# Steps 0 to 12 of the final stream, set between the products of the last layer's second half

## The chip, the cores and the metric

The kernel runs on one core of a Trainium2 chip. The metric is the device time of one execution in microseconds. A core has five engines that run beside each other, each through its own list of instructions in the order written: TensorE (PE, matrix products and transposes into PSUM banks), VectorE (DVE), ScalarE (ACT), GpSimd (POOL) and SyncE (SP, which only issues transfers here). They are tied together by semaphores: an instruction that waits holds up all that stand behind it on its engine.

## The reference

Three models in a row over x of 2 sequences by 1024 tokens, each with a residual sum: a two-layer token transformer of width 192 with banded attention, a retention block of width 128, and a layer of 8 experts with one expert for each token.

```python
def _L0_tok_ref(call, ...):
    for l in range(L):
        a = _longformer_attn(x, att_mask, ...)
        x = _ln(x + a, g1[l], beta1[l])
        h = jax.nn.relu(x @ W1[l].T + b1[l]) @ W2[l].T + b2[l]
        x = _ln(x + h, g2[l], beta2[l])
    x = _ln(x, gf, betaf)
    return x @ Wc.T + bc

def _L0_attn_ref(x, ...):
    y = retention_core(layernorm(x, ln1_g, ln1_b), decay_logit, W_out, b_out, conv_w, conv_b)
    x = x + y
    h = layernorm(x, ln2_g, ln2_b)
    h = jax.nn.gelu(jnp.einsum('btd,hd->bth', h, W1) + b1, approximate=False)
    y = jnp.einsum('bth,dh->btd', h, W2) + b2
    return x + y

h = _L0_tok_ref(x, ...)
h = h + _L0_attn_ref(_layernorm(h, axis=-1), ...)
h = h + _L0_ffn_ref(_layernorm(h, axis=-1), ...)
```

## The kernel before

The tokens are cut into blocks of 128, eight (`NB`) for each of the two sequences, sixteen in all (`NN`). The layers run as four rounds, sequence 0 with layers 0 and 1, then sequence 1 with layers 0 and 1. A round ends with a stretch whose order is written out by hand as a list of pairs in `seq_c`; PE, DVE, ACT and POOL each walk the same list and do their own part of each pair:

- `("y", i)`: for i from 0 to 7 the attention's output product of a block, for i from 8 to 15 the second feed-forward product (PE, `y_block`, L1369, six products with `w2s` per block). DVE adds the residual and takes the statistics (L1084, L922 to L924), POOL raises the variance to the power -0.5 (L545).
- `("z", i)`: DVE normalizes (L928), POOL scales and shifts into `resid` (L551, L552).
- `("tr", i)`: PE transposes z for the next product.
- `("hid", i)`: a hidden product of 512 tokens (PE, L1575 and L1576, banks 6 and 7), and its Relu on ACT (L811).

A y block lies in bank i % 4, so four can be under way before a z must be done.

What the last round leaves in `resid` goes through the final stream, a software pipeline of 29 steps (`NN + DEPTH`, L1593 on PE, L1141 on DVE, L819 on ACT, L624 on POOL). In step t each stage takes the block that belongs to it: block t takes the final norm's statistics, block t-1 is normalized (z0), transposed on PE (L1607, L1608), scaled by ACT (L824, L825) and multiplied with `wca` and `wcb` (L1650, L1651), whose result ACT copies to `h0` (L842). Block t-4 is normalized and transposed (L1634), block t-5 goes through the state scan on DVE (L1185), block t-6 through the five-tap convolution (L1601, ten matmuls) and the state product (L1612), blocks t-8 to t-10 through the second norm (L1656) and the products m1 and m2 (L1627, L1619), block t-12 through the last norm (L1661), and block t-13 through the router's product (L1641). DVE's part of a step takes all statistics first, hands the variances to POOL for one power (L637), and normalizes with the power of the step before (L1193). Four times in the stream a group of blocks is routed (`choose`, `rank`, `place`), and POOL scatters the rows to DRAM. When all sixteen blocks are out there, SP loads expert tiles, and 23 tiles run through the experts.

All four engines begin the stream behind the last pair of the last round.

## Time and profile before

| | |
|---|---|
| Time, median of 3 runs | 917.97 us (917.25 to 919.37) |
| Time of the profiled execution | 919.02 us |
| Its span in the trace | 916.9 us |
| Busy in the span | PE 809.2 (88%), DVE 634.4 (69%), POOL 567.2 (62%), ACT 563.3 (61%) |
| Mean granted clock of TensorE | 0.953 of full speed |
| Chain that ended last | PE 59%, DVE 21%, issue 5%, SP's queue 4%, POOL 4%, ACT 4%, DMA 3% |

The page of the profile also shows the span in 40 slices of about 23 us each:

```profile
PE   5979998999999989989999899999998986887397
DVE  2769975547899655578997553689975436988454
PEclk8989998999999999999999999999999996997599
```

A digit is the busy share in tenths, and in the row PEclk the clock that TensorE was granted, in tenths of full speed. The last eight digits are the end of the last layer, the stream and the experts. The clock has two levels, 2.4 GHz (1.00 in the views) and 1.2 GHz (0.50).

In the rows below "idle before" in square brackets is the time that the engine stood still ahead of a row, and what ended it. A matmul's duration overlaps with the next one's, so what a group of matmuls costs is read from the start of one group to the start of the next.

### The profile page before, as it was taken

To read this page: it belongs to the slowest core of one execution; us is meant where nothing else is said; L and a number is where in the kernel's file an instruction comes from. 1 tells how busy PE (TensorE), PEld (TensorE's weight loads), DVE (VectorE), ACT (ScalarE), POOL (GpSimd) and SP (SyncE) were. 2 spreads that over 40 slices of the span, in tenths; PEclk is the share of its full clock that TensorE was granted. 3 is DMA by queue.
4 is the path that set the end of the run, shared out by engine and by line. 5 is a ranking of instruction groups with operands and counts; after the bars stand their busy time and mean duration, and the time that the engine had idled before them with its cause. 6 is when DMAs were issued, how large, how long until landed. Compare 5 with 4: busy or idle time off the path is not lost.

```text
span 916.9 us, 23665 instructions
## 1 busy us (share of the span) xinstructions
PE 809.2 (88%) x8467; PEld 617.3 (67%) x8467; DVE 634.4 (69%) x1959; ACT 563.3 (61%) x1559; POOL 567.2 (62%) x820
## 2 busy tenths in 40 slices
PE   5979998999999989989999899999998986887397
PEld 2757766576777666667776666677766664876397
DVE  2769975547899655578997553689975436988454
ACT  2858885437788853267888543778885423565164
POOL 3638885545388856475888554438885546759345
PEclk8989998999999999999999999999999996997599
DMA  2310000142000012430000024200000245001331
GB/s 65 105 47 3 4 13 11 58 139 77 6 4 3 13 35 87 114 92 26 3 3 14 11 81 116 79 5 4 3 3 2 79 121 205 1 3 41 93 103 39
DMA packets 38595, 43.84 MB, mean 48 GB/s; under 512 B 7162, under 2 KB 33881, under 8 KB 38345
## 3 DMA queue, kind: packets, MB, share of 16 engines
q1 hardware_dynamic: 18348, 19.40, 7.1%
q10 hardware_dynamic: 17860, 18.19, 6.7%
q0 software_dynamic: 2272, 4.74, 1.7%
q8 instruction: 69, 1.13, 0.5%
q14 instruction: 46, 0.38, 0.1%
HBM read 20.70 MB, written 21.59 MB: 46 GB/s over the span
## 4 chain that ended last, share of the span: by engine, by line
PE 59%; DVE 21%; issue 5%; SPq 4%; POOL 4%; ACT 4%; DMA 3%; POOLq 0%; DVEq 0%; ACTq 0%
PE bank L1369 7%; DVE p L1011 6%; DVE nmx L1002 5%; PE bank L1575 5%; PE bank L1457 5%; PE bank L1576 5%; PE bank L1506 4%; PE bank L1530 4%; PE bank L1395 3%; PE bank L1406 3%; PE bank L1460 2%; PE bank L1509 2%; PE bank L1680 2%; PE bank L1601 2%; PE bank L1689 2%
## 5 line engine op out<-in xcount | busy, mean ns | idle before, releaser
L573 POOL TENSOR_TENSOR p<-p 128x384 f16<-128x384 f32 (+1 forms) x320 | 283.8, 907 | 103.4 <-ACT p L746 98.7
L1002 DVE TENSOR_REDUCE nmx<-bank 128x1 f32<-128x384 f32 (+1 forms) x384 | 190.6, 511 | 20.7 <-PE bank L1460 16.2
L744 ACT ACTIVATE p<-bank 128x384 f32<-128x384 f32 (+1 forms) x384 | 170.9, 452 | 54.3 <-PE bank L1509 38.0
L1506 PE MATMUL bank<-stack 103*128 103x128 bf16 x1056 | 145.1, 222 | 5.6 <-DMA stack<-mtr 5.1
L746 ACT ACTIVATE p<-bank 128x384 f16<-128x384 f32 (+1 forms) x320 | 144.3, 451 | 0.0
L1509 PE MATMUL bank<-bandb,idb 128*128 128x128 bf16 x672 | 135.3, 222 | 0.0
L1530 PE MATMUL bank<-vst,p 128*128 128x49 bf16 x2112 | 115.8, 185 | 15.2 <-DVE p L1011 13.6
L1457 PE MATMUL bank<-stack 100*128 100x384 bf16 (+1 forms) x384 | 121.2, 316 | 7.3 <-DVE nmx L1002 2.9
L1530 PEld LDWEIGHTS bank<-vst,p 128*128 128x128 f16 x2112 | 89.5, 97 | 32.4 <-DVE p L1011 19.1
L1506 PEld LDWEIGHTS bank<-stack 103*128 103x128 bf16 x1056 | 88.3, 98 | 29.7 <-issue 14.5
L1460 PE MATMUL bank<-bandb,idb 128*128 128x128 bf16 x672 | 101.2, 220 | 0.0
L545 POOL TENSOR_TENSOR rstd<-ve,colc 128x1 f32<-128x1 f32 x64 | 35.2, 550 | 101.7 <-DVE ve L924 101.7
L1084 DVE TENSOR_TENSOR bank<-bank,resid 128x192 f32<-128x192 f32 x64 | 23.1, 361 | 82.8 <-PE bank L1369 82.8
L1460 PEld LDWEIGHTS bank<-bandb,idb 128*128 128x128 bf16 x672 | 66.0, 98 | 20.9 <-issue 0.8
L811 ACT ACTIVATE hid<-bank 128x512 f32<-128x512 f32 x48 | 28.7, 597 | 81.8 <-PE bank L1576 81.8
L758 ACT ACTIVATE stack<-bank 96x1024 bf16<-96x1024 bf16 x64 | 65.1, 1017 | 18.6 <-PE bank L1395 17.2
L1395 PE MATMUL bank<-idb,hid 128*96 128x128 bf16 x768 | 59.3, 221 | 10.1 <-POOL hid L590 5.2
L1369 PE MATMUL bank<-w2s,hid 128*128 128x192 f32 x384 | 65.1, 328 | 2.8 <-ACT hid L811 2.8
L1369 PEld LDWEIGHTS bank<-w2s,hid 128*128 128x128 f32 x384 | 62.3, 190 | 7.2 <-issue 7.2
L1395 PEld LDWEIGHTS bank<-idb,hid 128*96 128x96 bf16 x768 | 51.2, 124 | 23.4 <-issue 16.8
L1509 PEld LDWEIGHTS bank<-bandb,idb 128*128 128x128 bf16 x672 | 65.6, 98 | 0.7
L1011 DVE TENSOR_TENSOR p<-p 128x384 f16<-128x384 f32 (+1 forms) x64 | 63.2, 987 | 2.2
(253 smaller groups left out, 1818.0 us busy)
## 6 DMA issues: line engine op xcount, KB each, us to landing
xs<-zrow ACTq DMA_DIRECT2D x8, 2193.0 KB, 13.5
xt<-xs SPq DMA_DIRECT2D x23, 129.0 KB, 2.1
w2s<-in_w SPq DMA_DIRECT2D x4, 576.0 KB
mwbs<-in_mwb SPq DMA_DIRECT2D x1, 2064.0 KB, 8.5
mw2s<-in_mw SPq DMA_DIRECT2D x1, 2048.0 KB, 12.8
...
stack<-mtr SPq DMA_DIRECT2D x96, 3.0 KB
...
```

The source lines that it names most:

```text
L573: nc.gpsimd.tensor_tensor(p2[:, u % RING, 0:w], p32[:, u % RING, 0:w], p1[:, u % RING, 0:w], ALU.subtract).then_inc(p2_pool, 1)
L744: ins = nc.scalar.activation(p32[:, s % RING, 0:w], ps[2 + s % 3][:, 0:w], ACT.Exp)
L746: ins = nc.scalar.activation(p1[:, s % RING, 0:w], ps[2 + s % 3][:, 0:w], ACT.Exp)
L1002: nc.vector.tensor_reduce(nmx[:, vn % 3, h:h + 1], nat_bank(v)[:, 0:w], AX.X, ALU.max, negate=True).then_inc(max_done, 1)
L1011: nc.vector.tensor_tensor(p2[:, u % RING, 0:w], p32[:, u % RING, 0:w], p1[:, u % RING, 0:w], ALU.subtract).then_inc(p2_dve, 1)
L1369: ins = mm(y, hid[:, m, blk(n % BPC)], w2s[:, m, :], start=m == 0, stop=m == FF // P - 1)
L1395: ins = nc.tensor.transpose(psb[3 + (3 * b + g) % 2][0:NPIECE, blk(h)], nat[:, b % 2, g * HG + h, :], idb[:, :])
L1457: mm(s_ps[:, 0:len(win) * P], q, stack[0:K_NAT, H + h, blk(win[0], len(win))], start=True, stop=False)
L1460: ins = mm(s_ps[:, blk(i)], idb[:, :], bandb[:, 0 if m < n else 1, :], start=False, stop=(i, m) == edges[-1])
L1506: ins = mm(ps[2 + s % 3][:, blk(i)], stack[0:K_ALL, H + h, blk(m)], stack[0:K_ALL, h, blk(n)], start=True, stop=m == n)
L1509: ins = mm(ps[2 + s % 3][:, blk(i)], idb[:, :], bandb[:, 1 if m < n else 0, :], start=False, stop=True)
L1530: ins = mm(out_ps, pt[:, w % RING, blk(a)], vst[:, m, h, :], start=False, stop=i == HH - 1 and a == len(win) - 1 and pt is p2)
```

## The change

Steps 0 to 12 of the stream (`FILLED = 13`) are taken out of the loop behind the rounds and put into the list of the last round, by the table `STREAM`. There are three kinds of such steps: step 0, 1 and 2 at y9, y10 and y11, steps 3 to 8 at the six hidden products of the second half, and steps 9 to 12 at y12 to y15. Each step is cut in two. The pair `("head", t)` stands ahead of its y block or hidden product, `("rest", t)` behind it. DVE and POOL do their whole step at the head. PE's and ACT's heads hold the convolution, the first transposes, m1, m2 and the router's product, and their rests the product with `wca` and the transposes of blocks t-8 and t-12.

So that both can be under way, the banks change. In the second half of the last round a y block takes bank i % 2, and y10 to y15 wait for z of the block two before instead of four before. The stream takes banks 2 to 7 where it took 0, 1, 3, 4, 6 and 7, the router's product moves from bank 5 to 0 and `rank` from 2 to 1, and the scaled blocks go to `ata` and `atb` instead of `xa` and `xb`. First uses of banks get a wait for what was there. The stream's small tiles lie in front of the experts' in memory now. The step functions are the loop bodies of before; the diff is cut to what differs and to PE's part in full.

```diff
+FILLED = 13
...
+        def y_bank(i, last):
+
+            return ps[i % 2 if last and i >= NB else i % 4][:, 0:D]
...
+            def stream(t):
...
+                        if kind == "head":
+                            stream(j)
...
+            def stream_head(t):
+                if t == 0:
+                    nc.scalar.activation(gs[0:1, 0, 0:1], lfa[0:1, 0:1], ACT.Gelu)
+                i = t - 1
+                if 0 <= i < NN:
+                    act.wait_ge(t0_mm, i + 1)
+                    nc.scalar.activation(ata[:, blk(i % NB)], ps[4][0:DLO, 0:P], ACT.Identity, bias=lfa[:, 1:2],
...
+            def stream_rest(t):
+                i = t - 1
+                if 0 <= i < NN:
+                    act.wait_ge(hw_mm, i + 1)
+                    nc.scalar.activation(h0[:, i, :], ps[2][:, 0:DM], ACT.Copy).then_inc(kept, 1)
...
+                        if kind == "head":
+                            stream_head(i)
+                        if kind == "rest":
+                            stream_rest(i)
...
-                        y = ps[i % 4][:, 0:D]
+                        y = y_bank(i, rnd == B * L - 1)
...
+                        if kind == "head":
+                            stream(i)
...
             def y_block(i):
                 n = block_of(i)
+                last = rnd == B * L - 1
                 if i >= 4:
-                    pe.wait_ge(z_ready, at(z_ready, i - 3))
-                y = ps[i % 4][:, 0:D]
+                    pe.wait_ge(z_ready, at(z_ready, i - 1 if last and i >= NB + 2 else i - 3))
+                y = y_bank(i, last)
...
+            def stream_head(t):
+                i = t - 6
+                if 0 <= i < NN:
+                    b, n = divmod(i, NB)
+                    pe.wait_ge(a1_done, min(i + 2, (b + 1) * NB))
+                    if i:
+                        pe.wait_ge(y_added, i)
+                    else:
+                        pe.wait_ge(z_ready, START[z_ready.num][B * L - 1] + NB)
+                    for k in range(KC):
+                        mm(ps[3][:, 0:DM], xn[:, b, n * P + k:(n + 1) * P + k], diag[:, k, :], start=k == 0, stop=False)
+                i = t - 1
+                if 0 <= i < NN:
+                    pe.wait_ge(z0_ready, i + 1)
+                    if i == 0:
+                        pe.wait_ge(ln_out, START[ln_out.num][B * L - 1] + NB)
+                    if t - 9 >= 0:
+                        pe.wait_ge(a2_done, t - 8)
+                    nc.tensor.transpose(ps[4][0:DLO, 0:P], z0[:, i % 2, 0:DLO], idf[:, :])
+                    nc.tensor.transpose(ps[4][0:DHI, P:2 * P], z0[:, i % 2, DLO:D], idf[:, :]).then_inc(t0_mm, 1)
+                i = t - 6
+                if 0 <= i < NN:
+                    pe.wait_ge(scan_done, i + 1)
+                    mm(ps[3][:, 0:DM], st[:, i % 4, :], wos[:, :], start=False, stop=True).then_inc(c_mm, 1)
+                i = t - 10
+                if 0 <= i < NN:
+                    pe.wait_ge(gelu_done, i + 1)
+                    if i:
+                        pe.wait_ge(x_added, i)
+                    else:
+                        pe.wait_ge(h_relu, START[h_relu.num][B * L])
+                    for m in range(2):
+                        ins = mm(ps[7][:, 0:DM], gl[:, i % 2, m, :], aw2s[:, m, :], start=m == 0, stop=m == 1)
+                    ins.then_inc(m2_mm, 1)
+                i = t - 9
+                if 0 <= i < NN:
+                    pe.wait_ge(a2_done, i + 1)
+                    if i:
+                        pe.wait_ge(gelu_done, i)
+                    else:
+                        pe.wait_ge(h_relu, START[h_relu.num][B * L] - 1)
+                    for m in range(2):
+                        ins = mm(ps[6][:, blk(m)], aw1s[:, m * P:(m + 1) * P], ht[:, i % 2, :], start=True, stop=True)
+                    ins.then_inc(m1_mm, 1)
+                i = t - 4
+                if 0 <= i < NN:
+                    pe.wait_ge(z1_ready, i + 1)
+                    if t - 13 >= 0:
+                        pe.wait_ge(a3_done, t - 12)
+                    nc.tensor.transpose(ps[5][:, 0:P], z1[:, i % 2, :], idf[:, :]).then_inc(t1_mm, 1)
+                i = t - 13
+                if 0 <= i < NN:
+                    pe.wait_ge(a3_done, i + 1)
+                    if i == 0:
+                        pe.wait_ge(z_ready, START[z_ready.num][B * L])
+                    for g, (a, _) in enumerate(GROUPS):
+                        if g and i == a:
+                            pe.wait_ge(lg_read, g)
+                    ins = mm(ps[0][:, i * E:(i + 1) * E], xm[:, i % 2, :], wgs[:, :], start=True, stop=True)
+                    if i + 1 in [e for _, e in GROUPS]:
+                        ins.then_inc(lg_mm, 1)
+
+            def stream_rest(t):
+                i = t - 1
+                if 0 <= i < NN:
+                    pe.wait_ge(a0_done, i + 1)
+                    if i:
+                        pe.wait_ge(kept, i)
+                    else:
+                        pe.wait_ge(z_ready, START[z_ready.num][B * L - 1] + NB - 1)
+                    mm(ps[2][:, 0:DM], ata[:, blk(i % NB)], wca[:, :], start=True, stop=False)
+                    mm(ps[2][:, 0:DM], atb[0:DHI + 1, blk(i % NB)], wcb[0:DHI + 1, :], start=False, stop=True).then_inc(hw_mm, 1)
+                i = t - 8
+                if 0 <= i < NN:
+                    pe.wait_ge(z2_ready, i + 1)
+                    pe.wait_ge(a0_done, min(t, NN))
+                    nc.tensor.transpose(ps[4][:, 0:P], z2[:, i % 2, :], idf[:, :]).then_inc(t2_mm, 1)
+                i = t - 12
+                if 0 <= i < NN:
+                    pe.wait_ge(z3_ready, i + 1)
+                    pe.wait_ge(a1_done, min(t - 3, NN))
+                    nc.tensor.transpose(ps[5][:, 0:P], trow[:, i, 0:DM], idf[:, :]).then_inc(t3_mm, 1)
...
-            for t in range(NN + DEPTH):
...
+            for t in range(FILLED, NN + DEPTH):
+                stream_head(t)
+                stream_rest(t)
...
+STREAM = {("y", 9): (0,), ("y", 10): (1,), ("y", 11): (2,), ("hid", 6): (3,), ("hid", 7): (4,), ("hid", 8): (5,),
+          ("hid", 9): (6,), ("hid", 10): (7,), ("hid", 11): (8,), ("y", 12): (9,), ("y", 13): (10,), ("y", 14): (11,),
+          ("y", 15): (12,)}
+
+
 def seq_c(rnd):
+    if rnd == B * L - 1:
+        seq = []
+        for kind, i in _seq_c():
+            if kind == "tr" and i >= NB:
+                continue
+            steps = STREAM.get((kind, i), ())
+            seq += [("head", t) for t in steps]
+            seq.append((kind, i))
+            seq += [("rest", t) for t in steps]
+        return seq
     last = rnd % L == L - 1
     seq = []
     for kind, i in _seq_c():
```

PE's list from y9 to the first hidden product. In it `bank0<-w2s,hid` with two rows is a y block, `z0` the normalized block of a step, `wca,ata` the product of its transposes. Before:

```order
L1369 MATMUL bank1<-w2s,hid 128x192 [waits h_relu,z_ready]
L1369 MATMUL bank1<-w2s,hid 128x192 x5
L1369 MATMUL bank2<-w2s,hid 128x192 [waits h_relu,z_ready]
L1369 MATMUL bank2<-w2s,hid 128x192 x5
L1369 MATMUL bank3<-w2s,hid 128x192 [waits h_relu,z_ready]
L1369 MATMUL bank3<-w2s,hid 128x192 x5
L1575 MATMUL bank6<-xa,w1a 128x512 [waits h_relu,ln_out]
L1576 MATMUL bank6<-xb,w1b 128x512
```

After (y9, head 1, y10, rest 1, head 2, y11; L1398 is the y block's line now):

```order
L1398 MATMUL bank1<-w2s,hid 128x192 [waits h_relu,z_ready]
L1398 MATMUL bank1<-w2s,hid 128x192 x5
L1419 MATMUL bank4<-idf,z0 96x128 [waits ln_out,z0_ready]
L1420 MATMUL bank4<-idf,z0 96x128
L1398 MATMUL bank0<-w2s,hid 128x192 [waits h_relu,z_ready]
L1398 MATMUL bank0<-w2s,hid 128x192 x5
L1471 MATMUL bank2<-wca,ata 128x128 [waits z_ready,a0_done]
L1472 MATMUL bank2<-wcb,atb 128x128
L1419 MATMUL bank4<-idf,z0 96x128 [waits z0_ready]
L1420 MATMUL bank4<-idf,z0 96x128
L1398 MATMUL bank1<-w2s,hid 128x192 [waits h_relu,z_ready]
L1398 MATMUL bank1<-w2s,hid 128x192 x5
```

The transposes of z0 and the product with `wca` stand between the y blocks now, and y10 is in bank 0 where y8 was.

DVE's list from the second half's second y block on. Before (y9, z8, y10):

```order
L1084 TENSOR_TENSOR bank<-bank,resid 128x192 [waits resid_ready,y_mm]
L922 BN_STATS bnst<-bank 128x6 [waits dve_own]
L923 BN_AGGR mv<-bnst 128x2 [waits dve_own]
L924 TENSOR_SCALAR ve<-mv 128x1 [waits dve_own]
L928 TENSOR_SCALAR zt<-bank,mv,rstd 128x192 [waits y_rstd,resid_ready,z_mm]
L1084 TENSOR_TENSOR bank<-bank,resid 128x192 [waits resid_ready,y_mm]
```

After, from the end of step 0 over y9 and z8 to z0 of step 1 (L974 to L1010 are the stream's lines):

```order
L992 TENSOR_SCALAR vin<-mean 128x1
L1187 TENSOR_TENSOR bank<-bank,resid 128x192 [waits resid_ready,y_mm]
L944 BN_STATS bnst<-bank 128x6 [waits dve_own]
L945 BN_AGGR mv<-bnst 128x2 [waits dve_own]
L946 TENSOR_SCALAR ve<-mv 128x1 [waits dve_own]
L950 TENSOR_SCALAR zt<-bank,mv,rstd 128x192 [waits y_rstd,resid_ready,z_mm]
L974 BN_STATS sums<-resid 128x6 [waits resid_ready]
L989 BN_AGGR mean<-sums 128x2 [waits dve_own]
L989 BN_AGGR mean<-sums 128x2 x3
L991 TENSOR_SCALAR vin<-mean 128x4 [waits dve_own]
L992 TENSOR_SCALAR vin<-mean 128x1
L1010 TENSOR_SCALAR z<-resid,mean,rs 128x192 [waits rs_ready]
```

Step 1's statistics and z0 stand behind y9 and z8 now, and step 0's between y8 and y9.

PE's list at y14 and y15 before, with the first product of the stream behind them:

```order
L1369 MATMUL bank2<-w2s,hid 128x192 [waits h_relu,z_ready]
L1369 MATMUL bank2<-w2s,hid 128x192 x5
L1369 MATMUL bank3<-w2s,hid 128x192 [waits h_relu,z_ready]
L1369 MATMUL bank3<-w2s,hid 128x192 x5
L1607 MATMUL bank0<-idf,z0 96x128 [waits z0_ready]
L1608 MATMUL bank0<-idf,z0 96x128
L1650 MATMUL bank6<-wca,xa 128x128 [waits a0_done]
```

After, from the convolution of head 11 to y14:

```order
L1411 MATMUL bank3<-diag,xn 128x128 [waits y_added,a1_done]
L1411 MATMUL bank3<-diag,xn 128x128 x4
L1419 MATMUL bank4<-idf,z0 96x128 [waits a2_done,z0_ready]
L1420 MATMUL bank4<-idf,z0 96x128
L1424 MATMUL bank3<-wos,st 128x128 [waits scan_done]
L1433 MATMUL bank7<-aw2s,gl 128x128 [waits x_added,gelu_done]
L1433 MATMUL bank7<-aw2s,gl 128x128
L1443 MATMUL bank6<-ht,aw1s 128x128 [waits gelu_done,a2_done]
L1443 MATMUL bank6<-ht,aw1s 128x128
L1450 MATMUL bank5<-idf,z1 128x128 [waits z1_ready]
L1398 MATMUL bank0<-w2s,hid 128x192 [waits h_relu,z_ready]
```

Between y13 and y14 PE now has a whole head, whose first row waits for DVE's add of step 11 (`y_added`) and whose transposes wait for its `z0`, and y14 stands behind all of it.

## Rows read from the trace of the kernel before

**Rows 1.** Timeline of PE: start us, duration us, what, idle before.

```profile
727.42 8.04 PE L1369 MATMUL bank<-w2s,hid 128*128 128x192 f32 x48 [0.34 <-ACT hid L811]
...
735.30 1.02 PE L1575 MATMUL bank<-xa,w1a 96*128 96x512 f32 x2
...
761.00 0.45 PE L1607 MATMUL bank<-idf,z 128*96 128x128 f32 x1 [6.41 <-DVE z L1193]
...
799.20 1.34 PE L1601 MATMUL bank<-diag,xn 128*128 128x128 f32 x10
800.38 0.27 PE L1607 MATMUL bank<-idf,z 128*96 128x128 f32 x1
```

**Rows 2.** Busy time in the stretch of steps 1 to 12: PE, PEld, DVE, ACT, POOL, clock.

```profile
761.00:799.20 38.20, 31.19 (x199) 26.70 (x200) 29.92 (x158) 19.55 (x58) 24.79 (x36) 0.79 0.22 83
```

**Rows 3.** Timeline of DVE at y11, z10 and z11.

```profile
735.50 0.37 DVE L1084 TENSOR_TENSOR bank<-bank,resid 128x192 f32<-128x192 f32 x1 [0.34 <-PE bank L1369]
...
736.63 0.48 DVE L928 TENSOR_SCALAR zt<-bank,mv,rstd 128x192 f32<-128x192 f32 x1
737.43 0.48 DVE L928 TENSOR_SCALAR zt<-bank,mv,rstd 128x192 f32<-128x192 f32 x1 [0.33 <-POOL rstd L545]
```

**Rows 4.** Timeline of DVE: steps 0 and 2 of the stream.

```profile
757.10 0.07 DVE L1097 MEMSET vin<- 128x10 f32 x1
...
758.80 0.14 DVE L1175 TENSOR_SCALAR vin<-mean 128x1 f32<-128x1 f32 x1
...
760.86 0.35 DVE L1157 BATCH_NORM_STATS2 sums<-resid 128x6 f32<-128x192 f32 x1
...
761.81 0.37 DVE L1193 TENSOR_SCALAR z<-resid,mean,rs 128x192 f32<-128x192 f32 x1
```

**Rows 5.** Timeline of DVE: first add and z0 of steps 10 and 14.

```profile
786.14 0.29 DVE L1147 TENSOR_TENSOR x<-bank,x 128x128 f32<-128x128 f32 x1
...
788.07 0.35 DVE L1193 TENSOR_SCALAR z<-resid,mean,rs 128x192 f32<-128x192 f32 x1
...
801.17 0.29 DVE L1147 TENSOR_TENSOR x<-bank,x 128x128 f32<-128x128 f32 x1
...
803.59 0.35 DVE L1193 TENSOR_SCALAR z<-resid,mean,rs 128x192 f32<-128x192 f32 x1
```

**Rows 6.** Timeline of PE: a convolution at low clock, a step at full clock.

```profile
773.83 2.34 PE L1601 MATMUL bank<-diag,xn 128*128 128x128 f32 x10
775.96 0.42 PE L1607 MATMUL bank<-idf,z 128*96 128x128 f32 x1
...
796.41 0.27 PE L1607 MATMUL bank<-idf,z 128*96 128x128 f32 x1
...
796.85 0.61 PE L1619 MATMUL bank<-aw2s,gl 128*128 128x128 f32 x4
...
797.86 0.39 PE L1650 MATMUL bank<-wca,xa 96*128 96x128 f32 x2
...
798.30 0.28 PE L1656 MATMUL bank<-idf,z 128*128 128x128 f32 x1
```

**Rows 7.** Windows: busy times; the third last figure is the granted clock.

```profile
61.00:66.00 5.00, 4.42 (x30) 3.23 (x30) 2.25 (x5) 2.99 (x11) 2.38 (x4) 0.50 0.01 1
393.00:400.00 7.00, 5.02 (x39) 3.15 (x38) 3.67 (x10) 4.46 (x9) 6.26 (x13) 1.00 0.27 74
579.00:582.00 3.00, 3.00 (x20) 2.39 (x19) 1.85 (x5) 2.34 (x5) 0.64 (x2) 0.50 0.18 60
760.00:776.00 16.00, 10.97 (x43) 8.67 (x44) 9.67 (x53) 6.08 (x17) 10.44 (x13) 0.50 0.59 221
```

**Rows 8.** Timeline of PE: gaps elsewhere in the program.

```profile
61.58 0.39 PE L1506 MATMUL bank<-stack 103*128 103x128 bf16 x2 [4.74 <-DMA stack<-mtr]
...
395.87 0.62 PE L1395 MATMUL bank<-idb,hid 128*96 128x128 bf16 x8 [1.98 <-POOL hid L590]
...
577.71 0.62 PE L1395 MATMUL bank<-idb,hid 128*96 128x128 bf16 x8 [1.60 <-POOL hid L590]
```

355 lines of the change are left out of this document (145 added, 210 removed).

## The prediction, made before the changed kernel ran

> **What bounds the kernel now.** I read the timeline of TensorE (PE) first, since the change moves its work, from the first feed-forward product of the last layer's second half to the experts [rows 1]. Here y8 to y11 (L1369) start at 727.42 and the six hidden products after them at 735.30, so a y block costs 7.88 / 4 = 1.97 us. The engine is nearly full until y15 ends at 754.59 (761.00 less 6.41). Then come 6.41 us without a matmul, until VectorE (DVE) has the first row of the stream: that idle time is what one would like to fill. The stream's step 13 begins on PE at 799.20 and its z transpose (L1607, which I call T0) at 800.38. **All steps that move lie between 754.6 and 799.2, 44.6 us**, and all that stands behind T0 of step 13 is unchanged. The question is only when that T0 comes.
>
> The stage view [rows 2] shows two engines nearly full in those 38.2 us of steps: PE 31.2 and DVE 29.9. That speaks against a simple overlap. A step is no spare PE work. It is a chain DVE, POOL, DVE, PE, ScalarE (ACT), PE. The DVE timeline gives the pieces: a y block's add, statistics and epsilon take 1.13 us until its neighbour's z can start [rows 3], begin 0.20 after PE is done (735.50 against 735.30), and a z takes 0.48, or 1.28 for the last two of a group, where the second waits for POOL's power. Steps 0, 1 and 2 [rows 4]: step 0 takes DVE 757.10 to 758.95, 1.85 us; a small step takes 1.32 from its first statistic (760.86) to the end of its z (762.18). A step 7 to 10 takes 2.29 from its first add to the end of z0 (786.14 to 788.43), one from 11 on 2.7 (801.17 to 803.95, less a pause of 0.1) [rows 5].
>
> **What the change costs, with the clock as it is now.** Every head is put ahead of a y block on both engines. So PE's y10 stands behind T0 of step 1, T0 waits for z0 of DVE's step 1, and that stands behind DVE's y9, which waits for PE's y9. In the order of before the y blocks ran back to back and DVE followed. Now each y block waits for DVE's answer to the y block before it. I walk along it.
> - y8 ends on PE at 727.42 + 1.97 = 729.39. DVE: 0.20, y8 1.13, step 0 1.85, y9 1.13, z8 0.48, step 1 1.32, which gives 735.50. T0 at 735.55, two transposes 0.22 (half of the 0.44 from 796.41 to 796.85 [rows 6]), y10 at 735.77. PE has done nothing since 731.36: **a gap of 4.19 us**.
> - y10 to y11: 1.97 + 0.20 + 1.13 + 0.48 + 1.32 + 0.05 + 0.22 = 5.37. y11 runs 741.14 to 743.11.
> - y11 to the hidden products: 0.20 + 1.13 + 1.28 + step 3 (1.32, and 0.27 for a second statistic) + 0.05 + 0.22 = 4.48. They start at 747.59 and not at 735.30, 12.3 us late for three steps.
> - Here the overlap is real. A hidden product is 1.72 us of PE (10.32 / 6) that needs no DVE, and ACT's copies of T0 hide behind it. The convolution is 1.18 (799.20 to 800.38 [rows 1]), T0 0.22, the state product 0.22, m2, m1 and one transpose 1.01 together (796.85 to 797.86), so some 0.45, 0.45 and 0.11, the two products of T0's copies 0.44 (797.86 to 798.30) [rows 6]. Hidden 10.32, rests of steps 3 to 8 2.75, heads 4 to 8 5.85, head 9 2.18: 21.1 us. DVE needs 1.6 (step 3) to some 3.2 (step 8, z0 at 2.29 and three more of 0.3) beside PE's 2.4 to 4.0, so PE sets the time. y12 starts at 768.7.
> - y12 to y15 stand against steps 10, 11 and 12. y12 to y13: 1.97 + 0.20 + 1.13 + 2.29 + 0.05 + 1.45 (T0 to the end of the head, 796.41 to 797.86 [rows 6]) = 7.1. The next two: 1.97 + 0.20 + 1.13 + 0.48 + 2.7 + 0.05 + 1.45 = 8.0 each. The convolution and the rests fit into this, and so do ACT and POOL, which were busy for 19.6 and 24.8 us of 38.2 in the steps alone [rows 2]. y15 ends at 768.7 + 7.1 + 16.0 + 1.97 = 793.8.
> - From there 0.20 + 1.13 + 1.28 + 0.1 (three small fills) + 2.7 + 0.05: T0 of step 13 at 799.2 against 800.4, **a gain of 1.2 us** out of 44.6.
>
> Costed at nothing: the bank numbers; the activation tables (one load for Gelu, as before); the copies to ata and atb for xa and xb; the queues. ACT issues its two fills of xs ahead of step 1's copies, which come 6 us later. SP's three loads of expert weights wait for the last y block and so start 39 us later, near 794. They are wanted after the last routing step, some 50 us behind step 13's T0; a load longer than that would hold up the experts, us for us.
>
> The Trainium skill (Perfetto Trace Analysis, Optimization Strategy) says that regimes with different busiest engines may gain from being interleaved. By it the PE work of steps 0 to 12 would go where PE waits. The stage rows speak against it here: DVE is as full in the steps as PE, and the order hands each y block the other engine's latency.
>
> **The clock.** A gap of 4.19 us is new, and one of about 2.7 us follows behind y10, one of 3.8 behind y11. Each loop of y12 to y15 holds some 1.5 and 1.2 us of idle time with the convolution between. What rows show of such gaps [rows 7, 8]: after 4.74 us (until 61.58) the granted clock was 0.50; after 6.41 it was 0.50 from 760 to 776; after 1.60 us (577.71) it was 0.50 from 579 to 582; after 1.98 us (395.87) it stayed at 1.00. So after 4.19 us I take 1.2 GHz as near certain and for the later loops as about even. The price: ten convolution matmuls span 2.13 us at the low level (773.83 to 775.96 [rows 6]) and 1.18 at the full one, nearly double.
> - y10 and y11 at half speed: 2 x 1.97, and the T0 pairs 2 x 0.22: **+4.4**. The rests lie in gaps.
> - The hidden products start low. In the solid work from 773.83 the level rose at about 776.9, so a low stretch of 3.4 us in solid work: **+1.7**. If it lasts twice as long, +3.4.
> - In y12 to y15 one more such stretch, of which PE works two thirds: **+1.1**. Bounds: none, 0; every loop low, 3 x 3.4 (1.97 + 1.45 doubled) = +10.
>
> The Trainium skill (TensorE: Matmul & The Clock Gate, Why this matters for your kernels) advises against idle gaps between bursts of matmuls, since the clock drops. The trace agrees at 4.74 and 6.41 us and shows a drop at 1.60 too, so I do not rely on the page's size of gap.
>
> **Sum.** -1.2 + 4.4 + 1.7 + 1.1 = +6.0 us. The profiled execution took 919.02 (span 916.9), which gives 925.0; it lies 1.05 above the median of 917.97, so on the scale of the medians **924.0 us**.
>
> **Rivals.**
> - The clock holds, or drops once and briefly. Then only -1.2 to +1 remains: 916.8 to 919. For it: the gap of 1.98 us left the clock alone. Against it: this gap is twice as long, 4.19 us in one piece, and two more follow. It decides at y10: if y10 lasts 1.97 us, this is the case. With the sum off by 0.7 us it is faster than before, and so it is the case on the other side of slower.
> - The overlap works as meant: DVE's z is there before PE asks, and PE's own work sets the end. PE's work in steps 0 to 12 is 12 x (0.22 + 0.44), 7 convolutions and states at 1.40, 9 + 5 + 1 transposes at 0.11 and 7 m products at 0.45: 22.5 us. With 754.6 and DVE's 5.5 us behind y15 that puts T0 of step 13 at 782.6, 17.8 earlier: 900 us. It needs y10 not to stand behind T0 of step 1; the order of the instructions says that it does.
> - The clock stays low through the second half too: y12 to y15 in loops of 11.4 us instead of 8.0, +10 in place of +1.1: 930 to 933.
> - DVE has slack in the loops that I did not see (adds that run while PE still works on the y block): up to 0.5 us in each of six loops, 3 us less with the clock as forecast: 921.
>
> **Chances.** Forecast with its neighbours (920 to 929): 0.60. Clock holds or nearly: 0.18, split evenly over its bound, since 0.2% is 1.84 us, about what a measurement of this kernel can tell from no change. Low throughout, over 929: 0.10. Overlap as meant or another gain of over 2 us: 0.12. So faster 0.20 (0.12 and 0.08 of the clock that holds), same 0.15 (the other 0.10, and 0.05 of the forecast's neighbours), slower 0.65. The range 915.5 to 930.5 leaves out the overlap as meant and the worst of the low clock. The forecast's own range is 920 to 928.
>
> **What would show it.** y9 on PE followed by about 4 us of idle time put down to DVE's z; y10 lasting near 3.9 us and a granted clock of 0.5 around 736 to 750; the first hidden product 12 to 17 us later than 735.3; y12 to y15 starting 7 to 8 us or more apart, with DVE's first add of a step directly behind its y block; then steps of about 4 us as before. Wrong would be a y10 that starts right behind y9, or a T0 of step 13 before 795 or behind 812.

## The result, and the profile after

The changed kernel takes 925.67 us (median of 4 runs, 923.50 to 927.12); the kernel before took 917.61 beside it (4 runs, 914.34 to 919.37). The ratio is 1.009, with a 95% interval of 1.0053 to 1.0127: **8.1 us slower**. The prediction was 924.0, slower, 6.0 us more. The profiled execution took 923.50, its span is 921.3.

By the two profiles the whole of it lies in one stretch, from the start of y8 to T0 (the z transpose on TensorE, PE) of step 16. In the timeline of PE of the changed kernel (start us, duration us, what, idle time before it and what ended it; T0 is now L1419, the y block L1398, the hidden product L1691):

```profile
723.39 4.14 PE L1398 MATMUL bank<-w2s,hid 128*128 128x192 f32 x24 [0.34 <-ACT hid L859]
731.22 0.45 PE L1419 MATMUL bank<-idf,z 128*96 128x128 f32 x1 [3.69 <-DVE z L1010]
...
738.45 0.45 PE L1419 MATMUL bank<-idf,z 128*96 128x128 f32 x1 [2.77 <-DVE z L1010]
...
746.68 0.45 PE L1419 MATMUL bank<-idf,z 128*96 128x128 f32 x1 [3.98 <-DVE z L1010]
...
747.14 1.92 PE L1691 MATMUL bank<-xa,w1a 96*128 96x512 f32 x2
...
770.26 2.12 PE L1398 MATMUL bank<-w2s,hid 128*128 128x192 f32 x12
...
777.54 2.12 PE L1398 MATMUL bank<-w2s,hid 128*128 128x192 f32 x12
...
785.74 2.12 PE L1398 MATMUL bank<-w2s,hid 128*128 128x192 f32 x12
...
795.11 2.57 PE L1398 MATMUL bank<-w2s,hid 128*128 128x192 f32 x12
...
803.49 0.45 PE L1419 MATMUL bank<-idf,z 128*96 128x128 f32 x1 [1.54 <-DVE z L1010]
...
808.75 0.27 PE L1419 MATMUL bank<-idf,z 128*96 128x128 f32 x1
...
816.69 0.27 PE L1419 MATMUL bank<-idf,z 128*96 128x128 f32 x1
```

and of the kernel before, y12 and T0 of steps 14 and 16 (y8 and step 13 are in [rows 1]):

```profile
746.56 3.65 PE L1369 MATMUL bank<-w2s,hid 128*128 128x192 f32 x21 [0.78 <-ACT hid L811]
...
804.35 0.27 PE L1607 MATMUL bank<-idf,z 128*96 128x128 f32 x1
...
812.28 0.27 PE L1607 MATMUL bank<-idf,z 128*96 128x128 f32 x1
```

From y8 to T0 of step 16 it was 812.28 - 727.42 = 84.9 us and is 816.69 - 723.39 = 93.3: 8.4 us more. Behind that T0 both kernels need the same 104.6 us (916.9 - 812.28 and 921.3 - 816.69), so the expert weights, which SyncE now fetches from 797.71 us on instead of 754.63, hold up nobody. Ahead of y8, where the two programs do the same, the changed kernel happens to be 4 us earlier in its profile; y8 started between 721.1 and 729.9 in the profiles of this study. That scatter is why a stretch is compared below, beside the time of the whole.

The busy times of the stretch from y8 to T0 of step 13 say it shortest (start:end, length, then busy us of PE, PE's weight loads, DVE, ACT, POOL, granted clock, DMA share, GB/s), before first:

```profile
727.42:800.38 72.96, 58.77 (x330) 47.88 (x330) 46.09 (x223) 26.33 (x71) 41.37 (x63) 0.88 0.39 127
```

```profile
723.39:803.49 80.10, 58.73 (x330) 49.54 (x330) 47.28 (x223) 26.00 (x71) 40.32 (x63) 0.89 0.24 74
```

The same 330 matmuls keep PE busy for the same 58.8 us, and it stands idle for 21.4 us instead of 14.2. Nothing was overlapped on balance; idle time was only moved, and 7 us added. The granted clock is 0.88 before and 0.89 after. So the changed kernel does not do more of this work at the low level than the kernel before, which had its low stretch in the first steps of the stream (0.50 from 760 to 776, [rows 7]); it does it in other places. What is called the price of the clock below is therefore counted against the changed kernel at full clock, and not against the kernel before. The waits of PE in the changed kernel from 723 to 808 name what it waits for:

```profile
PE bank L1419 <- DVE z L1010: 15.2, 7, 4.0
PE bank L1411 <- DVE x L964: 6.1, 4, 2.2
```

Seven waits for VectorE's (DVE's) z0 and four for its add (L964) ahead of the convolution (L1411), 21.3 us. Both stand in DVE's order behind its work on a y block. At y13, in the timeline of DVE (add of y13, add of step 11, z0 of step 11):

```profile
779.70 0.37 DVE L1187 TENSOR_TENSOR bank<-bank,resid 128x192 f32<-128x192 f32 x1 [2.90 <-PE bank L1398]
...
781.22 0.28 DVE L964 TENSOR_TENSOR x<-bank,x 128x128 f32<-128x128 f32 x1
...
783.76 0.44 DVE L1010 TENSOR_SCALAR z<-resid,mean,rs 128x192 f32<-128x192 f32 x1
```

DVE first idles for 2.90 us for PE's y13, and then PE idles for DVE. Behind y15 it is the same, and there DVE's part is the longer one: the add of y15, the add of step 13 and z0 of step 13, for which T0 of step 13 waits:

```profile
797.72 0.37 DVE L1187 TENSOR_TENSOR bank<-bank,resid 128x192 f32<-128x192 f32 x1 [4.31 <-PE bank L1398]
...
800.16 0.28 DVE L964 TENSOR_TENSOR x<-bank,x 128x128 f32<-128x128 f32 x1
...
802.99 0.44 DVE L1010 TENSOR_SCALAR z<-resid,mean,rs 128x192 f32<-128x192 f32 x1
```

The granted clock (the third figure from the end) in y10, and in y15 with its head:

```profile
731.20:735.20 4.00, 3.98 (x16) 3.97 (x17) 0.00 (x0) 0.80 (x2) 1.01 (x1) 0.58 1.09 305
...
792.44:797.50 5.06, 5.06 (x25) 5.06 (x26) 0.97 (x4) 1.77 (x5) 1.01 (x1) 0.66 0.00 0
```

### The profile page after: what moved, and what is told of

Read it like the earlier page. It is cut to its first block, busy times and chain, and to the rows that moved or that the text cites. A ratio compares the mean times of both kernels' runs of the same rounds, so it can differ in the third digit from the quotient of the medians.

```text
span 921.3 us, 23671 instructions
## 1 busy us (share of the span) xinstructions
PE 808.4 (88%) x8467; PEld 619.2 (67%) x8467; DVE 636.3 (69%) x1959; ACT 562.6 (61%) x1559; POOL 567.6 (62%) x820
## 4 chain that ended last, share of the span: by engine, by line
PE 59%; DVE 23%; issue 5%; SPq 4%; POOL 4%; ACT 3%; DMA 2%; POOLq 0%; DVEq 0%; ACTq 0%
PE bank L1398 7%; DVE p L1114 6%; PE bank L1569 5%; PE bank L1691 5%; PE bank L1692 5%; DVE nmx L1105 4%; PE bank L1618 4%; PE bank L1642 4%; PE bank L1507 3%; PE bank L1518 3%; PE bank L1572 2%; PE bank L1621 2%; PE bank L1730 2%; PE bank L1739 2%; SPq L462 2%
## 5 line engine op out<-in xcount | busy, mean ns | idle before, releaser
L1187 DVE TENSOR_TENSOR bank<-bank,resid 128x192 f32<-128x192 f32 x64 | 23.1, 361 | 90.6 <-PE bank L1398 90.6
L1398 PE MATMUL bank<-w2s,hid 128*128 128x192 f32 x384 | 69.0, 338 | 2.0 <-ACT hid L859 2.0
L1398 PEld LDWEIGHTS bank<-w2s,hid 128*128 128x128 f32 x384 | 65.6, 199 | 5.6 <-issue 5.6
```

The costliest lines, as they stand in the source:

```text
L1398: ins = mm(y, hid[:, m, blk(n % BPC)], w2s[:, m, :], start=m == 0, stop=m == FF // P - 1)
```

## The experiments

My theory: the place of the steps in the order makes a closed loop of PE and DVE at every y block (each waits for the other's last piece of work), and its gaps lower the clock. The rivals: the pair of PSUM banks that the y blocks now share holds them; or a step's own chain is too long for this place, whatever the order. All kernels at one glance; the stretch goes from y8 to T0 of step 16 in each one's profile, the last column is the ratio to the kernel before, measured on the same chip in the same rounds. The runs were made on several chips, and the median of the kernel before lay between 917.1 and 922.9 us beside them. So medians of different rows are compared by their ratios, or put on the scale of 917.6 us.

| kernel | y8, T0 of 16 | stretch us | against before | ratio (95%) |
|---|---|---|---|---|
| before | 727.42, 812.28 | 84.9 | | |
| changed | 723.39, 816.69 | 93.3 | +8.4 | 1.009 (1.0053 to 1.0127) |
| vector ahead | 726.20, 797.54 | 71.3 | -13.5 | 0.9837 (0.9799 to 0.9876) |
| third bank | 723.45, 816.68 | 93.2 | +8.4 | 1.0081 (1.0046 to 1.0115) |
| gaps filled | 729.26, 820.37 | 91.1 | +6.3 | 1.0033 (1.0006 to 1.006) |
| hidden only | 726.62, 805.12 | 78.5 | -6.4 | 0.9897 (0.9839 to 0.9954) |
| ahead, third bank | 721.08, 789.29 | 68.2 | -16.7 | 0.9792 (0.9739 to 0.9844) |
| gaps fitted | 729.92, 818.23 | 88.3 | +3.5 | 1.005 (1.0024 to 1.0076) |
| banks alone | 726.27, 819.17 | 92.9 | +8.0 | 1.0109 (1.0053 to 1.0166) |
| two ahead | 726.06, 795.45 | 69.4 | -15.5 | 0.9859 (0.9812 to 0.9906) |
| ahead late | 723.55, 804.46 | 80.9 | -4.0 | 0.9933 (0.9913 to 0.9953) |
| ahead early | 727.39, 811.76 | 84.4 | -0.5 | 0.9992 (0.9966 to 1.0017) |
| first two ahead | 729.65, 798.30 | 68.7 | -16.2 | 0.9799 (0.9766 to 0.9832) |

1% is 9.2 us. The stretch tells the ratio within its interval for all but two, the filled gaps and ahead late, and there it is outside by 1 us or less.

### DVE and POOL one item ahead

The two changed loops are those of DVE and POOL (GpSimd) alone; the table says ahead of which pair each step stands in their lists. The code is cut to these places.

```diff
+AHEAD = {("y", 8): (0,), ("y", 9): (1,), ("y", 10): (2,), ("y", 11): (3,), ("hid", 6): (4,), ("hid", 7): (5,),
+         ("hid", 8): (6,), ("hid", 9): (7,), ("hid", 10): (8,), ("hid", 11): (9,), ("y", 12): (10,), ("y", 13): (11,),
+         ("y", 14): (12,), ("y", 15): (13,)}
...
-def seq_c(rnd):
+def seq_c(rnd, STREAM=STREAM):
...
-                    for kind, i in seq_c(rnd):
+                    for kind, i in seq_c(rnd, AHEAD):
...
-            for t in range(FILLED, NN + DEPTH):
+            for t in range(FILLED + 1, NN + DEPTH):
```

> As the changed kernel, but VectorE (DVE) and GpSimd (POOL) take each step of the stream one item earlier: step 0 ahead of their y8, step 1 ahead of y9, ... step 13 ahead of y15. TensorE (PE) and ScalarE (ACT) keep their order. My theory (the place of the step in DVE's order costs the time: PE's y block waits for T0, T0 for DVE's z0, and that stands behind DVE's work on the y block before): the gap of 3.7 us ahead of y10 and those of 2.8 and 4.0 behind it shrink to under 2 us, y12 to y15 follow each other in 5 to 5.5 us instead of 7.3 to 9.4, the clock stays up, and from y8 to T0 of step 13 it is 53 to 58 us instead of 79.7. Time 898 to 908, taken 902. Rival 1 (the two banks that the y blocks share hold them, each waits for the z of the block before last): y8 to y11 stay as they are, 3.7 us of gap, and only y12 to y15 gain, 2 us each: 915 to 919. Rival 2 (the steps' own chain of DVE, POOL, PE and ACT is too long for one item, whatever the order): y12 to y15 stay at 7 to 8 us, 920 to 926.

906.76 us, ratio 0.9837; on the scale of 917.6 that is 902.6. PE's timeline from y10 to T0 of step 13:

```profile
732.39 2.22 PE L1398 MATMUL bank<-w2s,hid 128*128 128x192 f32 x12 [1.09 <-DVE zt L950]
...
742.97 0.31 PE L1419 MATMUL bank<-idf,z 128*96 128x128 f32 x1 [1.61 <-DVE z L1010]
...
768.53 2.12 PE L1398 MATMUL bank<-w2s,hid 128*128 128x192 f32 x12
...
773.60 2.12 PE L1398 MATMUL bank<-w2s,hid 128*128 128x192 f32 x12
...
779.24 2.22 PE L1398 MATMUL bank<-w2s,hid 128*128 128x192 f32 x12 [0.41 <-DVE zt L950]
...
783.07 0.27 PE L1419 MATMUL bank<-idf,z 128*96 128x128 f32 x1
```

y13 to y14 takes 5.07 us instead of 8.20, without a wait on PE, and from y8 to T0 of step 13 it is 56.9 us instead of 80.1. The two engines do the same work as in the changed kernel, and PE's order is the same to the instruction: only DVE and POOL take a step ahead of a y block's add instead of behind it. So the theory holds, and the rival of a chain that is too long falls. In this run 3.1 us of waits for z0 are left of 15.2, and none for the add. DVE and POOL were moved together; which of the two would do alone was not tested. What is new is small: y10 and y11 wait 1.09 and 1.03 us for z8 and z9 (L950), that is, for a bank; and 6.5 us instead of 4.0 lie between T0 of steps 13 and 14 (783.07 to 789.56), since step 14 of DVE stands behind y15, z14 and z15. I had expected the clock to stay up throughout, and it did not: behind the gap of 1.61 us it fell, and from T0 of step 4 to that of step 5 it took 3.96 us.

### A third bank, in the changed kernel

```diff
-            return ps[i % 2 if last and i >= NB else i % 4][:, 0:D]
+            return ps[(0, 1, 3, 0)[i - NB] if last and NB <= i < NB + 4 else i % 2 if last and i >= NB else i % 4][:, 0:D]
...
-                    pe.wait_ge(z_ready, at(z_ready, i - 1 if last and i >= NB + 2 else i - 3))
+                    pe.wait_ge(z_ready, at(z_ready, (i - 1 if i > NB + 4 else i if i == NB + 4 else i - 2) if last and i >= NB + 2 else i - 3))
```

> As the changed kernel, but y8 to y11 turn over three PSUM banks instead of two, and wait for the z of the third block before them, not the second. Theory (the order holds y10 and y11, not the banks): T0 of the step ahead of y10 waits longer than the bank did, so the gap ahead of it stays at 3.7 us and the time at 924 to 927. Rival (the pair of banks holds them): y10 follows y9 within 0.5 us, y11 likewise; 5 to 9 us less with the clock held up, 917 to 920.

928.96 us, ratio 1.0081, which is 925.0 on the scale of 917.6. T0 of steps 1 and 13:

```profile
731.28 0.45 PE L1419 MATMUL bank<-idf,z 128*96 128x128 f32 x1 [3.69 <-DVE z L1010]
...
803.47 0.45 PE L1419 MATMUL bank<-idf,z 128*96 128x128 f32 x1 [1.54 <-DVE z L1010]
```

The gap is 3.69 us as in the changed kernel, and the stretch is the same within 0.1. In the changed kernel's order the pair of banks does not hold y10 and y11. The third bank was given to y8 to y11 alone; for y12 to y15 it is the trace of the changed kernel that speaks, where no y block waits for a z (L950).

### The gaps filled with idle work, twice

```diff
+                            if i in (1, 2, 3):
+                                pe.wait_ge(ln_out, START[ln_out.num][B * L - 1] + NB)
+                                fill = (10, 7, 11)[i - 1]
+                                for k in range(fill):
+                                    mm(ps[5][:, 0:D], idf[:, :], w2s[:, k % 6, :], start=k == 0, stop=k == fill - 1)
                             stream_head(i)
```

In the first of the two, 14 stood in place of fill.

> As the changed kernel, but ahead of T0 of steps 1, 2 and 3 PE runs 14 products of 128x192 (2.3 us at full clock) whose result nobody reads, so that the three gaps of 3.7, 2.8 and 4.0 us are mostly filled. It adds work and takes no wait away. Theory (the clock's share of my sum: 4.4 us for y10, y11 and T0 at half speed and 1.7 for the first hidden product): granted clock 1.00 from y9 to the hidden products, y10 and y11 2.0 us instead of 3.5, the hidden products start 3 to 4 us earlier, 919 to 922, taken 920.5. Rival (the clock's low stretches lie where DVE sets the time anyway, or the gaps left over still lower it): 924 to 928.

926.98 us, ratio 1.0033, which is 920.6 on the scale of 917.6 and by number what I had expected. The profile does not show what I expected, though. The clock did stay up (1.00 in y10, which shows 2.12 us), but the hidden products started 23.1 us behind y8, hardly earlier than in the changed kernel (23.8), and the stretch is only 2.2 us shorter. So the number that fits is luck in part; this is one of the two rows in which stretch and ratio disagree. I had the length of the filling wrong: 14 such products take 4.6 us and not 2.3, more than any gap, so PE came late to T0 by its own work:

```profile
737.78 0.27 PE L1419 MATMUL bank<-idf,z 128*96 128x128 f32 x1
```

It has no idle time before it. So I fitted them.

> As the filled gaps, but with 10, 7 and 11 products in the three gaps (3.3, 2.3 and 3.6 us at full clock) in place of 14 each, which had taken 4.6 us and more than the gap: there T0 came right behind them. Theory (the clock's term of the sum is 4.4 and 1.7 us): each gap keeps its length of 3.2 to 4.4 us, y10 and y11 take 2.0 us, and from y8 to T0 of step 13 it is 74 to 76 us instead of 80.1; ratio 1.002 to 1.004 (919.5 to 921). Rival (idle time of under 0.5 us left over, or a low stretch further on, takes it back): over 78 us, ratio 1.007 and more.

922.14 us, ratio 1.005. T0 of steps 1 and 2, and the clock in y10:

```profile
737.77 0.32 PE L1419 MATMUL bank<-idf,z 128*96 128x128 f32 x1 [0.45 <-DVE z L1010]
...
743.37 0.32 PE L1419 MATMUL bank<-idf,z 128*96 128x128 f32 x1 [0.50 <-DVE z L1010]
```

```profile
738.00:740.20 2.20, 2.20 (x16) 2.20 (x15) 0.02 (x1) 0.80 (x2) 0.76 (x1) 1.00 1.08 338
```

The clock is 1.00 where it was 0.58, and from T0 of step 1 to that of step 2 it takes 5.60 us instead of 7.23. From y8 to T0 of step 9 (770.33 - 729.92) it is 40.4 us instead of 45.9 (769.26 - 723.39). **The clock's price in the first half is 5.5 us**, measured by 28 products that compute nothing; I had charged 6.1. Up to T0 of step 13 the 5.5 us remain (74.6 us against 80.1): the low stretch at y15 came one block earlier, at y14, which lasts 2.45 us where it lasted 2.12, and cost as much there. Over the whole stretch 5.0 us remain, since T0 of step 14 comes 5.72 us behind that of step 13 and not 5.26. The ratio is a little over what I expected, and its interval covers that. The interval (up to 1.0076) overlaps that of the changed kernel (from 1.0053), so it is the stretch that gives the price. The gaps themselves stayed, as they must, since no wait was taken away.

### Only the steps beside the hidden products

```diff
-FILLED = 13
+FILLED = 6
...
+STREAM = {("hid", 6): (0,), ("hid", 7): (1,), ("hid", 8): (2,), ("hid", 9): (3,), ("hid", 10): (4,), ("hid", 11): (5,)}
...
-            return ps[i % 2 if last and i >= NB else i % 4][:, 0:D]
+            return ps[(0, 1, 3)[(i - NB) % 3] if last and i >= NB else i % 4][:, 0:D]
...
-                    pe.wait_ge(z_ready, at(z_ready, i - 1 if last and i >= NB + 2 else i - 3))
+                    pe.wait_ge(z_ready, at(z_ready, i - 2 if last and i >= NB + 2 else i - 3))
```

> Of the change only what lies beside the hidden products: steps 0 to 5 stand at the six hidden products 6 to 11, no step stands at a y block, steps 6 on follow behind y15, and y8 to y15 turn over three banks. Theory (the overlap is real beside the hidden products and lost at the y blocks): y8 to y11 run back to back in 7.9 us, the hidden products with their steps take 14 to 15 us instead of 10.3, y15 ends near 758, T0 of step 6 comes 10 to 13 us earlier than before (775.96), and some 1 to 3 us of that are lost to a low clock behind the gap: 904 to 909 against 917.6 before, taken 906. Rival (steps among other products cost more than they save wherever they stand, since each waits for the other engines' answers): 915 to 925.

914.42 us, ratio 0.9897, which is 908.2 on the scale of 917.6. So steps beside the hidden products, by themselves and with a third bank, gain about what the whole change loses. But the hidden products with their steps took 20.9 us (734.52 to 755.44) and not 14 to 15, and T0 of step 6 came 41.5 us behind y8 (768.14 - 726.62) instead of 48.5, which is 7.0 us and not 10 to 13. The reason stands at its first step, and at T0 of step 6 behind y15:

```profile
741.09 0.45 PE L1419 MATMUL bank<-idf,z 128*96 128x128 f32 x1 [4.69 <-DVE z L1010]
...
766.09 1.35 PE L1411 MATMUL bank<-diag,xn 128*128 128x128 f32 x10 [2.60 <-DVE zt L950]
```

DVE's steps 0 and 1 stand behind its y11, z10 and z11, so PE waits 4.69 us for the first z0 even here, and then the next hidden product runs at the low level (1.91 us instead of 1.02 for its first half). It is the same wait for DVE's answer once, instead of at each y block.

### The bank numbers alone

```diff
-FILLED = 13
+FILLED = 0
...
+STREAM = {}
```

> The other part alone: no step of the stream is moved, all of them stand behind y15 as before, but with the new banks, so y8 to y15 share two. Theory (a y block then waits for the z of the block before last, 0.20 + 1.13 + 0.48 us behind the end of its neighbour): gaps of 1.8 us ahead of y10, y11, y14 and y15, 7 us in all, 923 to 927 against 917.6. In the changed kernel the same wait lies inside the longer wait for T0 and costs nothing. Rival (which is what I charged in the sum: the bank numbers cost nothing): 916 to 919.

927.63 us, ratio 1.0109; on the scale of 917.6 that is 927.6, 0.6 above what I expected. y10 and y14 on PE:

```profile
732.11 2.22 PE L1398 MATMUL bank<-w2s,hid 128*128 128x192 f32 x12 [1.70 <-DVE zt L950]
...
755.18 2.22 PE L1398 MATMUL bank<-w2s,hid 128*128 128x192 f32 x12 [1.70 <-DVE zt L950]
```

Four gaps of 1.70 us. y8 to y12 takes 23.07 us (749.34 - 726.27) where it took 19.14 before, and y12 to T0 of step 1 18.38 where it took 14.44, so a pair of gaps costs 3.9. **One half of the change alone costs as much as the change.** It doesn't add to the other half: where PE waits for T0 anyway, the bank has long been free by then, as the third bank showed. Mend the order alone, and the bank becomes the next wait. The stream's own new bank numbers cost next to nothing: from T0 of step 1 to T0 of step 16 it is 51.5 us here and 51.3 before.

### Ahead, with the third bank

The edits of the first and the second experiment together.

> The first experiment (DVE and POOL one item ahead) with the third bank of the second one for y8 to y11. Theory (with the order mended, the pair of banks is what holds y10 and y11: there it ended their waits of 1.09 and 1.03 us): both waits go, DVE with 2.9 us a block is next, 1 to 2 us less than the first experiment's 0.984 of before: ratio 0.982, 901 on the scale of before's 917.6. Rival (DVE is as late as the bank): no change, 0.984.

896.68 us, ratio 0.9792, the lowest of all, though its interval overlaps those of the first experiment and of the first two ahead. T0 of steps 2 and 4:

```profile
728.79 0.31 PE L1419 MATMUL bank<-idf,z 128*96 128x128 f32 x1 [0.21 <-DVE z L1010]
...
736.34 0.31 PE L1419 MATMUL bank<-idf,z 128*96 128x128 f32 x1 [1.67 <-DVE z L1010]
```

The waits of y10 and y11 for banks are gone, and the stretch is 3.1 us shorter than with DVE and POOL ahead alone. 1.4 of these come at the second hidden product, where the clock stayed up this time (T0 of step 5 is 2.60 us behind that of step 4, not 3.96). So the same edit is worth nothing in one order and some 1.8 us in the other; 1.5 of these stand ahead of T0 of step 4, which comes 15.3 us behind y8 and not 16.8. The ratios alone could not tell so small a difference.

### Which loops cost how much

Ahead late has the table of the first experiment from step 9 on, and that of the changed kernel before (step 9 stands with step 8 at the last hidden product). Ahead early has it up to step 3.

> The first experiment cut in two, first half: DVE and POOL are ahead by one item at y12 to y15 alone (step 9 stands beside the last hidden product with step 8, step 13 ahead of y15); at y9 to y11 and the first hidden products they stand as in the changed kernel. Theory (each y block with a step ahead of it is a closed loop of its own, so the shares add): y12 to y15 follow each other in 5.1 us instead of 7.3, 8.2 and 9.4, T0 of step 13 stands 3.8 us behind the start of y15 instead of 8.4, 13 to 14 us together, of which 1.2 come back ahead of step 14: from y8 to T0 of step 16 80.4 us instead of 93.3, ratio 0.994. Rival (what is gained at the later blocks is wanted again by something that the first ones make late): over 84 us, ratio over 0.999.

> The other half: DVE and POOL are ahead at y8 to y11 alone, and from step 4 on they stand as in the changed kernel. Theory: gaps of 0.5, 1.1 and 1.0 us instead of 3.7, 2.8 and 4.0, y10 and y11 at full clock: 9 us less of the 93.3 from y8 to T0 of step 16, 84 us, ratio 0.998 to 0.999. With the other half the shares come to the 22 us of the whole. Rival (not additive): 88 us and more, or under 80.

912.34 us (0.9933) and 917.62 (0.9992). In the stretch the later blocks give 93.3 - 80.9 = 12.4 us and the earlier ones 93.3 - 84.4 = 8.9, together 21.3 of the 22.0 of the whole. The shares of the two halves add, as they should if each y block with a step ahead of it is a loop of its own. Ahead late has y14 5.07 us behind y13, as the first experiment has, and its T0 of step 1 waits as long as in the changed kernel:

```profile
731.39 0.45 PE L1419 MATMUL bank<-idf,z 128*96 128x128 f32 x1 [3.70 <-DVE z L1010]
...
775.43 2.12 PE L1398 MATMUL bank<-w2s,hid 128*128 128x192 f32 x12
...
780.50 2.12 PE L1398 MATMUL bank<-w2s,hid 128*128 128x192 f32 x12
```

### Further ahead

```diff
-AHEAD = {("y", 8): (0,), ("y", 9): (1,), ("y", 10): (2,), ("y", 11): (3,), ("hid", 6): (4,), ("hid", 7): (5,),
+AHEAD = {("y", 8): (0, 1), ("y", 9): (2,), ("y", 11): (3,), ("hid", 6): (4,), ("hid", 7): (5,),
```

Both kernels start from the one with DVE and POOL ahead and the third bank. "First two ahead" has this edit of the table alone, "two ahead" a second one with it, by which DVE and POOL take step 14 ahead of z15 and PE's first router product waits for z14 only:

```diff
-         ("y", 14): (12,), ("y", 15): (13,)}
+         ("y", 14): (12,), ("y", 15): (13,), ("z", 15): (14,)}
```

> The kernel of the third bank with DVE and POOL ahead, and more of the same: steps 0 and 1 both stand ahead of DVE's y8, step 2 ahead of y9, and step 14 stands ahead of z15 instead of behind it (TensorE's first routing product then waits for z14 only). Theory (DVE's place in the chain is still what costs at both ends): T0 of step 1 without a wait (0.54 us there), T0 of step 14 about 1 us earlier behind y15 (6.5 us lay between T0 of 13 and 14 instead of 4.0): 1 to 3 us less than with the third bank alone, ratio 0.979 to 0.981. Rival (PE is full there and nothing is gained): the same as the third bank alone.

> The third bank with DVE and POOL ahead, with only the first of the two further edits: steps 0 and 1 stand ahead of DVE's y8 and step 2 ahead of y9; step 14 is back behind z15. That run and the one with the third bank differ by 1.2 us in the stretch from y8 to T0 of step 16 (69.4 against 68.2). Theory (step 14 ahead of z15 cost it: it puts off z15, which step 15 needs, and a low stretch of the clock at the second hidden product cost 1 us more): 67.5 to 68.5 us here, ratio 0.978 to 0.984. Rival (the first two steps ahead are what cost): 69 us and more.

Two ahead: 904.06 us, ratio 0.9859; with the first two alone: 901.51, 0.9799. Neither beats the third bank's 0.9792. Step 14 ahead of z15 brings its T0 0.36 us nearer to that of step 13 (6.11 instead of 6.47) and puts off step 15's by 1.05 (5.06 instead of 4.01), since step 15 needs z15's residual: a loss of 0.7 us, where I had expected a gain of 1; the ratio of 0.9859 is above the 0.979 to 0.981 that I had written down. The first two steps ahead do gain: T0 of step 3 stands 9.8 us behind y8 (739.46 - 729.65) and not 11.0. But T0 of step 5 then comes 3.95 us behind that of step 4 and not 2.60, and the 1.2 us are gone. It is the clock. First two ahead, then the third bank, both from T0 of step 4:

```profile
743.70:747.60 3.90, 3.90 (x11) 2.21 (x12) 3.22 (x15) 1.71 (x4) 3.74 (x6) 0.65 0.27 65
```

```profile
736.34:741.00 4.66, 4.66 (x18) 2.62 (x19) 4.47 (x24) 2.96 (x8) 4.32 (x7) 1.00 0.04 12
```

At 68.7 us the stretch lies between my two bounds, so the rival isn't excluded by it; it is the distance to T0 of step 3 that speaks against it.

## Why the prediction was right

The mechanism was the one forecast, and most terms of the sum were near. Two terms of the clock were off in opposite directions, and one stretch behind y15 was missed. Times are counted from the start of y8, the forecast with its terms for the clock:

| point | forecast | measured |
|---|---|---|
| gap ahead of T0 of step 1 | 4.19 | 3.69 |
| first hidden product | 20.2 + 4.4 = 24.6 | 23.75 |
| its phase, to y12 | 21.1 + 1.7 = 22.8 | 23.1 |
| y12 to y13, y13 to y14 | 7.1, 8.0 | 7.28, 8.20 |
| y14 to y15, with the clock | 8.0 + 1.1 | 9.37 |
| T0 of step 13 | 71.8 + 7.2 = 79.0 | 80.1 |

- **The loop.** Each head on PE waits for DVE's answer to the y block before it: so it is, with 15.2 us of waits for z0 and 6.1 for the add, and DVE and POOL ahead took away all but 3.1 of them. The place of a step in the lists of DVE and POOL is the cause, since that run changes nothing else; the overlap beside the hidden products is real, and the loops cost more than it gains. Without the clock I had the change at -1.2 us; measured are 8.4 less the clock's 5.5 and 1.2 (below), +1.7. Of the 2.9 us between them 2.2 stand behind y15, and 1.3 of these came with the clock low again. Both numbers set the new order at full clock against a kernel before that had a low stretch of its own; what that one cost was not measured.
- **The gap** was 0.5 us shorter: step 0 on DVE took 1.18 us behind y8 and not the 1.85 that I had from rows where it stood alone. The other pieces up to the hidden products took more than I had: with the gaps fitted they started 20.5 us behind y8, where I had 20.2 without the clock. That they started 0.8 us earlier than forecast in the changed kernel is due to the clock (below), not to the gap.

```profile
726.74 0.07 DVE L955 MEMSET vin<- 128x10 f32 x1
...
727.92 0.35 DVE L1187 TENSOR_TENSOR bank<-bank,resid 128x192 f32<-128x192 f32 x1
```

- **The clock** was charged with 6.1 us up to y12 and measured at 5.5. Two misses hide in this: up to the start of the hidden products I charged 4.4 and it took 3.2 (23.75 less 20.52), since y10 and y11 ran only in part at half speed (3.4 and 3.2 us, not 3.94); from there to y12 I charged 1.7 and it took 2.2 (23.12 less 20.89). My 3.4 us of low stretch was not what its row gives either: from 773.83 to 776.9 it is 3.1 us, which makes the term 1.5. In y12 to y15 I charged one low stretch with 1.1 and there was one, at y15, which made its loop 1.2 longer.
- **What I missed** lies behind y15. T0 of step 13 came 8.4 us behind the start of y15, where I had 7.4, because y15 took 0.4 us more at the low clock and DVE's step 13, from its first add to the end of z0, took 3.27 us (800.16 to 803.43) and not 2.7. T0 of step 14 came 5.26 us later and not 3.97, with the clock at 0.74 in between. The two make 2.2 us. I had let the new gaps end with y15, but the last of them, 2.24 and 1.54 us, stand at step 13.
- **Costed at nothing** were the bank numbers. That was right for this order, and for a wrong reason: I had not priced the shared pair at all. Alone it costs 8 us, and in the mended order 1.8. The expert weights and the queues cost nothing, as the equal 104.6 us at the end show.
- The forecast came to +6.0 us for the whole; measured are +8.4 in the stretch and +8.1 in the medians. The 924.0 looks nearer to 925.67 than it was, as the kernel before had a median of 917.61 beside it and not of 917.97.

Of the rivals, the one where the overlap works as meant had 900 us, with the condition that y10 doesn't stand behind T0 of step 1. That condition was too strict. In the first experiment y10 still stands behind T0 of step 1 on PE, and the time is 902.6 on that scale: it is enough that T0 doesn't wait for DVE's work on y9. The price was nearly right, and the changed kernel's order kept it from coming true. That the clock holds was decided at y10, as the text said: it lasted 3.4 us (731.68 to 735.07) and not 2.0.

The Trainium skill (Perfetto Trace Analysis, Optimization Strategy) says that interleaving regimes with different busiest engines may improve performance. The changed kernel shows no such gain, and the first experiment shows 13.5 us: in these traces interleaving paid where the engines that feed the step run ahead.

## What to carry to other kernels

When a chain of steps over several engines is laid between the items of another chain, write down for each engine which of the two it takes first. If every engine takes the step ahead of the item, an item can come to wait for another engine's answer to the item before it, and the engines take turns, as they did here; let the engine that produces the step's input run one item ahead and the same instructions can overlap. And price a shared buffer in the order that is to come, not in the one that is there: here it was worth nothing, 1.8 us or 8 us by what else was being waited for.

## What the runs showed of the chip

- A gap on PE does not tell by its length whether the clock falls. Behind 1.67 us ahead of T0 of step 4 it stayed at 1.00 with the third bank; behind 1.65 us at the same place in the program it was 0.65 over the next 3.9 us, which cost 1.35 us, and behind 1.61 in the first experiment it was low too (3.96 us to T0 of step 5). The four gaps of 1.70 us of the banks alone left y10, y11, y14 and y15 at 2.22 us each, at full speed. Behind the gaps of 2.77, 3.69, 3.98 and 4.69 us the next work began at the low level each time (0.61, 0.58, 0.50 and 0.50 over the next 3 to 5 us). Behind gaps of 2.24 us (T0 of step 13 of the changed kernel, ahead of it the convolution) and 2.60 us (step 6 of hidden only) the convolution ran at full speed, 1.35 us, and the level fell only behind it. What decides between the two I have not tested.
- 10, 7 and 11 products that compute nothing, laid into gaps of PE, made the stretch 5.0 us shorter (88.3 us against 93.3), by the clock, since no wait was taken away. The ratios (1.005 against 1.009) point the same way, and their intervals overlap.
- The same wait costs more than its length: in the banks alone a pair of gaps of 1.70 us costs 3.9 us, since work ahead of a gap is paid to the end of its last matmul: y8 and y9 show 4.14 us and cost 3.94 where the next matmul follows at once, and a y block behind such a gap shows 2.22 us where one without a gap shows 2.12.
